# Two projections of an expert taken in turns by quarter: order of TensorE's work in a two-layer transformer kernel

## The reference

```python
xn = (x - mu) * rsqrt(var + EPS) * ln_g + ln_b
abel = gelu(xn @ abel_w + abel_b)
logits = xn @ gate_w_moe + gate_b_moe            # top 2 of 8, softmax -> wdense
h = gelu(einsum('bsd,edf->besf', xn, w1) + b1)   # 128 -> 512 channels, every expert
eo = einsum('besf,efd->besd', h, w2) + b2        # 512 -> 128
moe = einsum('besd,bse->bsd', eo, wdense)
nonabel = moe @ rot
g = sigmoid(concat([abel, nonabel]) @ mix_w + mix_b)
out = x + abel * (1 - g) + nonabel * g
```

## Time and profile before

| | us |
|---|---|
| median of 3 runs (865.5, 869.27, 881.5) | 869.27 |
| the profiled execution | 877.47 |
| its span, first to last instruction | 875.7 |
| busy in the span: PE / DVE / ACT / POOL | 697.6 / 670.6 / 501.6 / 114.5 |
| mean granted TensorE clock (1 is full) | 0.865 |

### The profile page before, as it was taken

The page is one execution under the profiler, slowest core; times in us unless marked ns, Lnnn a source line. Parts: engine busy times, 40 slices in busy tenths (PEclk is TensorE's granted clock), DMA queues, the critical chain, the costliest instruction groups (busy, mean ns, idle before and its releaser), DMA issues. The chain is left out here.

```text
span 875.7 us, 14793 instructions
## 1 busy us (share of the span) xinstructions
PE 697.6 (80%) x5418; PEld 549.5 (63%) x5418; DVE 670.6 (77%) x1464; ACT 501.6 (57%) x926; POOL 114.5 (13%) x91
## 2 busy tenths in 40 slices
PE   6375766666377899999999767788887869999996
PEld 4255655555375667778778544455454448888886
DVE  3998899999935797989979856887777137777765
ACT  4767576877525476866768425675665524234232
POOL 1113122213303560000000063000000000000000
PEclk9987787867675998999989867998888669999998
DMA  7453333444403411003020040000000000000000
GB/s 229 115 139 105 93 111 102 117 112 133 120 26 111 137 49 63 35 1 98 1 65 33 0 145 1 1 1 1 2 1 1 1 1 1 1 13 1 13 13 12
DMA packets 76699, 48.30 MB, mean 55 GB/s; under 512 B 54994, under 2 KB 64980, under 8 KB 76628
## 3 DMA queue, kind: packets, MB, share of 16 engines
q1 hardware_dynamic: 73268, 44.75, 17.5%
q10 hardware_dynamic: 3360, 2.62, 1.0%
HBM read 37.85 MB, written 9.50 MB: 54 GB/s over the span
## 5 line engine op out<-in xcount | busy, mean ns | idle before, releaser
L918 ACT ACTIVATE hT<-hps,b1s 128x512 f32<-128x512 f32 x128 | 87.9, 692 | 63.4 <-PE hps L829 60.7
L1084 DVE TENSOR_TENSOR hl<-hT,hh 128x512 fp32r<-128x512 f32 x128 | 91.7, 738 | 29.6 <-ACT hh L924 28.0
L1492 DVE TENSOR_REDUCE mx<-s_ps 128x2 f32<-128x512 f32 x128 | 82.6, 688 | 39.2 <-PE s_ps L1263 38.5
L1428 ACT ACTIVATE pt<-st_ps 128x512 f32<-128x512 f32 x128 | 69.8, 603 | 42.2 <-PE st_ps L1273 42.0
L1693 ACT ACTIVATE act_h<-up 128x512 f32<-128x512 f32 x64 | 38.3, 598 | 89.7 <-PE up L1646 89.7
L313 ACT ACTIVATE rest<-rest,par 128x264 f32<-128x264 f32 x128 | 53.7, 502 | 36.8 <-DVE rest L561 36.8
L306 ACT ACTIVATE tap<-cst_s,par 128x328 f32<-128x328 f32 x128 | 72.3, 653 | 3.8 <-DVE par L614 3.8
L1777 DVE TENSOR_TENSOR hid<-act_h,up 128x512 f32<-128x512 f32 x64 | 43.3, 685 | 27.9 <-PE up L1646 17.1
L1657 PEld LDWEIGHTS eo<-wc,hid 128*128 128x128 f32 x512 | 61.7, 192 | 2.3
L1657 PE MATMUL eo<-wc,hid 128*128 128x128 f32 x512 | 62.1, 275 | 0.0
L924 ACT CAST hh<-hT 128x512 fp32r<-128x512 f32 x96 | 59.2, 617 | 0.0
(11 more groups left out here) (255 smaller groups left out, 1704.6 us busy)
## 6 DMA issues: line engine op xcount, KB each, us to landing
kd<-kst SPq DMA_DIRECT2D x16, 512.0 KB, 2.6
xc<-in_x_coarse SPq DMA_DIRECT2D x16, 512.0 KB, 4.0
wdB<-wdd SPq DMA_DIRECT2D x32, 256.0 KB, 5.2
dW<-kd SPq DMA_DIRECT2D x16, 256.0 KB, 3.3
Ks<-kd SPq DMA_DIRECT2D x64, 33.0 KB, 2.1
dW<-kd SPq DMA_DIRECT2D x64, 32.0 KB, 2.1
w1r<-in_w ACTq DMA_DIRECT2D x5, 256.0 KB, 2.7
w2r<-in_w ACTq DMA_DIRECT2D x5, 256.0 KB, 3.2
```

Source lines behind the costliest of these rows:

```text
L918: nc.scalar.activation(hT[k][:], hps[:, k, :], ACT.Gelu, bias=b1s[:, m:m + 1]).then_inc(h_done, 1)
L1084: nc.vector.tensor_tensor(hl[s % 2][:, k, :], hT[k][:], hh[s % 2][:, k, :].bitcast(F32), ALU.subtract).then_inc(hl_done, 1)
L1428: nc.scalar.activation(pt[h % 8][:].rearrange("p t q -> p (t q)"), st_ps[k][:], ACT.Exp, scale=SCALE)\
L1492: nc.vector.tensor_reduce(mx[:, :, h:h + 1], s_ps[k][:].rearrange("p (t k) -> p t k", t=2), AX, ALU.max).then_inc(s_used, 1)
```

## The change

`up` and `down` take a quarter k. In a step the first three quarters of `down(s-1)` are put between the quarters of `up(s)`; the fourth stays where the whole was, behind the small jobs of e = 0, 3 and 5. Waits and signals stay with their quarter: those for the tokens and the weights ahead of quarter 0 of `up`, that for `eo_used` ahead of quarter 0 of `down`, `down_ready` after quarter 3.

```diff
-            def up(s):
+            def up_quarter(s, k):
                 q, e = s // E, s % E
+                if s >= 1:
+                    pe.wait_ge(h_done, 4 * (s - 1) + k + 1)
+                for i, (w, x) in enumerate(((high, xnh), (high, xnl), (low, xnh))):
+                    last = nc.tensor.matmul(hps[:, k, :], w[e][0][:, k * P:(k + 1) * P], x[q % 2][:],
+                                            start=(i == 0), stop=(i == 2))
+                last.then_inc(up_ready, 1)
+
+            def up(s, k):
+                q, e = s // E, s % E
+                if k > 0:
+                    up_quarter(s, k)
+                    return
                 if e == 0:
                     pe.wait_ge(xnh_done, q + 1)
                     pe.wait_ge(xnl_done, q + 1)
                 if q == 0 and e >= 1:
                     pe.wait_ge(w_ready, e)
...
+                up_quarter(s, k)
+
+            def down(s, k):
                 e = s % E
-                if s >= 2:
+                if s >= 2 and k == 0:
                     pe.wait_ge(eo_used, s - 1)
...
+                pe.wait_ge(hl_done, 4 * s + k + 1)
+                for i, (w, x) in enumerate(((high, hh), (high, hl), (low, hh))):
+                    last = nc.tensor.matmul(eo[:, s % 2, :], w[e][1][:, k, :], x[s % 2][:, k, :],
+                                            start=(k == 0 and i == 0), stop=(k == 3 and i == 2))
+                if k == 3:
+                    last.then_inc(down_ready, 1)
 
             for s in range(STEPS):
                 q, e = s // E, s % E
-                up(s)
+                up(s, 0)
+                for k in range(3):
+                    if s >= 1:
+                        down(s - 1, k)
+                    up(s, k + 1)
...
                 if s >= 1:
-                    down(s - 1)
+                    down(s - 1, 3)
...
-            down(STEPS - 1)
+            for k in range(4):
+                down(STEPS - 1, k)
```

## The result

The changed kernel took a median of 886.15 us against 875.38 for the kernel before in the same comparison: a ratio of 1.0146, with a 95% interval of 1.0089 to 1.0203. (The ratio compares only executions in the faster of the kernel's two states, so it is not the quotient of these medians.) A second comparison on another occasion gave 1.0121 (1.0050 to 1.0191). The change makes the kernel slower by 11 to 13 us, where 7.3 had been forecast; whether it is slower by 2% is not decided. The direction and most of the places came as forecast, and 886.15 lies in the range of 864 to 889. The 876.6 itself was missed by 9.6, of which 6.1 is that the kernel before took 875.38 this time and not 869.27: that the range held owes something to its width. One term of the sum was much too small.

A forecast was written before the change was run, and what follows sets the result against it. TensorE and VectorE near their limit bound the kernel. Terms 1.2 + 2.2 + 2.2 + 1.2 - 0.4 + 0.9 = 7.3 us on 877.47 give 884.8, less 8.2 for the median: 876.6, range 864 to 889.

The forecast's parts named there:

- Two engines near their limit, no wait at the products, so the change can lose more than it wins: First FFN: TensorE busy 215.50, VectorE 197.40 of 232.00 us; only small waits to win, later data can stall TensorE.
- both rivals that had it faster or moved only the end: FFN loop: waits vanish unreplaced, -2.5 us, 866.8, chance 0.15; or order does not matter, 0.9, 870.2, chance 0.12.
- VectorE's order becomes the bound in every step: Rival: VectorE needs 5.9 us per step over a beat of 5.52; 0.4 x 28 = 11, 880.5, chance 0.09.
- Alternating itself costs nothing: Transitions between up- and down-products: 0 us, as 0.23 separates products either way; at most 17 over about 186 transitions.
- VectorE's lag of 1.27 gives stalls of 0.9, 0.9 and 1.2: Late low parts stall down-products at starts of steps 12, 20 (0.9 each) and 28 (1.2); lag carried from step 9.
- The wait at line 815 goes, and ScalarE's rows swallow it: Steps 12/13 and 20/21: 1.51 before transposes back goes; TensorE waits 2.6 for normalised rows; each place costs 2.2 us.
- Routing weights, the end: Wait of 0.4 us at line 799 goes, -0.4; after step 31 VectorE's last combination comes later, costing 0.9.
- First tokens 1.2: Wait for normalised rows in the first 512 tokens: high part 1.0 us later, with some slowed low parts 1.2.
- Steps 9, 17 and 25: nothing: Undisturbed steps: VectorE's later low parts stay covered before the down-products, so these steps grow by 0 us.
- The weight wait of 4 stays: TensorE's 4.1 us wait for GpSimd's weights stays, change 0, since the GELU that their loads follow has not moved.
- The clock rival: TensorE's clock falls behind six new stalls, 6 x 2.5 = 15 us more, 891.6; sign: loop clock off 0.93 by over 0.02; chance 0.12.
- The upper end of the likeliest case: Whole kernel: 881 us if each of the seven places costs 0.5 more than in the forecast of 876.6.

The follow-up runs named there:

- 7 to 10: Residual's product and sum (7, 8) or output statistics (9, 10) left out of kernel before (7, 9) and changed kernel (8, 10); step 12 in 10: 5.73 instead of 6.64.
- 9: Output row statistics (line 1057) left out of the kernel before; step 13 took 8.11 us, as with 8.12.
- 11: Changed kernel with ScalarE's normalised rows ahead of its fourth GELU; wait for them 2.44 to 1.37 us, steps 12 and 13 took 14.93.
- 2: Changed kernel with the first 512 tokens in blocks of twelve products as before; 1.0120 of the kernel before, steps 0 to 5 took 47.63 us.
- 5: Kernel before with weights of experts 3 to 7 neither loaded nor split, GpSimd idle in the loop; steps 2 to 5 took 25.16 us.
- 6: Changed kernel with weights of experts 3 to 7 neither loaded nor split, GpSimd idle in the loop; steps 2 to 5 took 26.60 us.
- halves: Up- and down-products alternate by two quarters instead of the changed kernel's one; 1.0004 of the kernel before, steps 12 and 13 took 14.81 us.
- experiment 1: The changed kernel run again unedited, giving its second trace; 1.0121 of the kernel before.
- run 12: Kernel before with small jobs of experts 0 and 5 behind the down-block and ScalarE's normalised rows ahead of its fourth GELU; 1.0005 of the kernel before.

## Why the prediction was right and where it was not

- *Two engines near their limit, no wait at the products, so the change can lose more than it wins*: right. The ratio's interval excludes both rivals that had it faster or moved only the end. The rival *VectorE's order becomes the bound in every step* had 11 us, close to what was measured, and only the lengths of the steps part it from the forecast: it wanted 0.4 more in each, and undisturbed ones grew by 0.06 or less.
- *Alternating itself costs nothing*: right within 0.06 per step. Steps 10 and 27 take 5.66 and 5.57 instead of 5.62 and 5.52; the bound of 17 us was far off.
- *VectorE's lag of 1.27 gives stalls of 0.9, 0.9 and 1.2*: 0.82, 0.85 and 1.13. The further 0.4 forecast for steps 13 and 21 did not come (no such wait over 0.15), and the rows' wait would have swallowed it. The number of the lag was right, its reason half so: the lag does not hang on the work since step 9, as ScalarE alone sets nearly the same one in step 10 (7 to 10).
- *The wait at line 815 goes, and ScalarE's rows swallow it*: right, 2.44 and 2.46 for 2.6, net 2.37 for 2.2. Shown from both sides, by 9 (VectorE's relief is swallowed in the order of before) and 11 (ScalarE relieved, TensorE gains 1.1).
- *Routing weights, the end*: -0.63 for -0.4, 1.06 for 0.9.
- *First tokens 1.2, "with some low parts slowed beside GpSimd there"*: this is the step that failed: 4.5 and 3.8 were measured, 2.6 to 3.3 more. The low parts beside GpSimd averaged 1.03 us instead of 0.69 and were in the trace; I took 2.07 us of lost cover for them as for any other step and worked no sum. Runs 2, 5 and 6 put the excess there. Of the second trace's, 1.5 is the half clock behind the wait of 3.01 in step 5.
- *Steps 9, 17 and 25: nothing*: 0.45 each, 1.4 in all. In steps 8, 16 and 24 the first low part stands behind the routing shares in VectorE's list; TensorE waits up to 0.18 for it at the start of steps 9, 17 and 25. The idle time that the view prints is less than what such a wait costs; the start of step 17 in the first trace:

```profile
405.21 0.40 PE L823 MATMUL hps<-xnh,w1l 128*128 128x512 f32 x1
405.76 0.47 PE L845 MATMUL eo<-hh,w2h 128*128 128x512 f32 x1 [0.16 <-DVE hl L1095]
406.07 0.40 PE L845 MATMUL eo<-hl,w2h 128*128 128x512 f32 x1
```

  The product starts 0.55 behind the one before it and the next 0.31 later, instead of 0.23 each: 0.40 in all. The 0.41 at line 799 that cost 0.63 in step 16 is of the same kind. I had looked for late low parts only behind the residual and the statistics. With halves these steps took 6.33 to 6.35 again.
- *The weight wait of 4 stays*: 0.57 in the first trace and 3.25 in the second; the cost shows as a wait for low parts instead (2.67 and none), so the sum was hardly touched.
- *The clock rival*: its sum of 15 us is refuted, and the mean of the loop stayed within the 0.02 that I had set as the sign. Its mechanism is there all the same: half clock for 3.4 us came behind one new wait of the first trace and behind two of the second, at 1.5 us each (experiment 1). The comparison with the 1.51 before, which had none behind it, did not carry over to the new waits of 2.4 and 3.0.
- *The upper end of the likeliest case*, 881: seven places at 0.5 on top of 876.6 make 880.1.

## What to carry to other kernels

Interleaving two streams on an engine that was already nearly gapless gained nothing there; it moved the last input of the one later and the first due time of the other earlier. For such a change, add up both shifts (here 2.07 and 2.07 us) and go through the neighbours' lists, work item by work item, asking which have less slack than that, and which only seem to have it because an unrelated wait covers them. Stretches in which a neighbour runs slower than usual need a sum of their own.

## What the runs showed of the hardware

VectorE beside GpSimd was slowed by kind of instruction, not throughout. In the first trace of the changed kernel the residual, which GpSimd's split of expert 3's weights now overlaps, takes 3.99 us for four, where before, ahead of the split, it took 1.13. These are rows of the changed kernel, then the row before:

```profile
291.87 3.99 DVE L1042 SCALAR_TENSOR_TENSOR base<-xh,twice,abel 128x128 f32<-128x128 f32 x4
```

```profile
288.68 1.13 DVE L1031 SCALAR_TENSOR_TENSOR base<-xh,twice,abel 128x128 f32<-128x128 f32 x4
```

(The second trace has its residual ahead of the split, at 1.14, and the same wait of 3.01 in step 5: that wait does not hang on the residual.)

And in steps 4 and 5 of the second trace, with GpSimd at work until 304.14 and from 306.20 to 310.42:

```profile
302.91 1.52 DVE L1094 CAST hh<-hT 128x512 fp32r<-128x512 f32 x1
...
307.30 0.74 DVE L1111 SCALAR_TENSOR_TENSOR part<-eo,b2c,wdB 128x512 f32<-128x512 f32 x1
308.08 1.22 DVE L1114 TENSOR_TENSOR acc<-acc,part 128x512 f32<-128x512 f32 x1
309.22 2.95 DVE L1095 TENSOR_TENSOR hl<-hT,hh 128x512 fp32r<-128x512 f32 x3
```

The combination, one of whose inputs lies in PSUM, keeps its 0.74; the sum and the low parts, with two inputs in SBUF, take 1.22 for 0.69 and about 0.98 for 0.63. The cast of a high part has one input and took 1.52 for 0.42, while a reduction with one input kept its 0.69 beside the split (at 296.91 in the first trace). The Trainium skill ("SBUF — State Buffer", "SBUF: two separate sides") says that a VectorE instruction in a two-port mode, or one with two SBUF inputs beside a GpSimd instruction that reads SBUF, competes with GpSimd for one pair of ports, and that whichever starts second waits for the whole of the other. These rows agree for the two-input instructions and for the combination's 0.74; whether the cast ran in such a mode no run here shows.

TensorE's clock was at its lower level in step 7, 15 or 23 in two of three groups before the change, and in all three groups of run 12, which also has blocks; both orders have it. In the traces of the kernel before, of the change and of run 12 it falls during the last of the small row products of the step before (lines 792 and 794), some 3 us after they began, and stays at 0.50 for 6.8 us, of which this is a part:

```profile
383.30:388.30 5.00, 5.00 (x12) 3.94 (x13) 1.51 (x11) 2.74 (x5) 0.00 (x0) 0.50 0.00 0
```

That is run 12; the earlier trace rows has the same of the kernel before. The price can be read there: steps 6 and 7, and 22 and 23, took 18.83 and 18.50 with such a stretch, steps 14 and 15 took 15.40 without, so it costs 3.1 to 3.4 us. It comes or stays away from one trace to the next, and is probably part of why whole times spread more than these effects.
